# A fused attention and FFN block on one core: last layer-norm step of four units on GpSimd, weight loads behind row transfers, all orders anew

## The reference

```python
qkv = (jnp.einsum('bnd,ed->bne', x, qkv_w) + qkv_b).reshape(b, n, H, 3 * HD)
attn = softmax(einsum('bhqd,bhkd->bhqk', q, k) * SCALE, axis=-1)
x = layernorm(x + (einsum('bnd,ed->bne', out, fc_w) + fc_b + x))
h = silu(tlin(x, w1_w, w1_s)) * tlin(x, w2_w, w2_s)
h = gelu(tlin(h, h1_w, h1_s), approximate=False)
h = gelu(tlin(h, h2_w, h2_s), approximate=False)
x = layernorm(x + tlin(h, w3_w, w3_s))
```

## Time and profile before

| | |
|---|---|
| median of 3 runs | 312.81 us (312.67 to 313.73) |
| the profiled execution | 313.6 us, of which 311.8 are the span from the first to the last instruction |
| TensorE busy | 290.1 us (93%) |
| VectorE busy | 249.6 us (80%) |
| ScalarE busy | 241.4 us (77%) |
| GpSimd busy | 143.4 us (46%) |
| granted TensorE clock, mean | 0.98 |

### The profile page before, as it was taken

The page is one execution under the profiler, slowest core; times in us unless marked ns, Lnnn a source line. Parts: engine busy times, 40 slices in busy tenths (PEclk is TensorE's granted clock), DMA queues, the critical chain, the costliest instruction groups (busy, mean ns, idle before and its releaser), DMA issues.

```text
span 311.8 us, 6746 instructions
## 1 busy us (share of the span) xinstructions
PE 290.1 (93%) x2337; PEld 167.9 (54%) x2337; DVE 249.6 (80%) x561; ACT 241.4 (77%) x458; POOL 143.4 (46%) x255
## 2 busy tenths in 40 slices
PE   8959699999999999999999999998999999999991
PEld 8733254456555546353444363454556568558980
DVE  0669779998989999798899868538998784658993
ACT  2744588898979998999999888989886896984440
POOL 5162679514628991606149816707493290000101
PEclk9979899999999999999999999999999999999996
DMA  5687410045641004403610034450100000010011
GB/s 156 192 149 166 151 37 5 4 65 72 107 68 35 4 0 69 71 5 47 93 52 4 2 55 85 67 78 10 34 4 3 2 3 2 2 36 0 3 34 38
DMA packets 20276, 15.67 MB, mean 50 GB/s; under 512 B 2945, under 2 KB 19090, under 8 KB 20242
## 3 DMA queue, kind: packets, MB, share of 16 engines
q1 hardware_dynamic: 20242, 15.22, 24.9%
HBM read 5.51 MB, written 1.05 MB: 21 GB/s over the span
## 4 chain that ended last, share of the span: by engine, by line
PE 65%; DVE 12%; ACT 8%; SPq 5%; issue 4%; DMA 3%; POOL 0%; POOLq 0%; DVEq 0%; ACTq 0%
PE bank L484 23%; PE bank L524 14%; PE bank L495 8%; PE bank L506 8%; DVE negmax L879 7%; SPq L382 4%; ACT prob L735 4%; PE bank L466 2%; PE bank L548 2%; DMA stack<-mT 2%; PE bank L477 2%; DMA stack<-parts 1%; PE bank L578 1%; PE bank L459 1%; PE bank L565 1%
## 5 line engine op out<-in xcount | busy, mean ns | idle before, releaser
L879 DVE TENSOR_REDUCE negmax<-bank 128x1 f32<-128x512 f32 x256 | 159.8, 682 | 29.9 <-PE bank L495 29.4
L735 ACT ACTIVATE prob<-bank 128x512 f32<-128x512 f32 x256 | 134.0, 618 | 9.1 <-PE bank L506 8.0
L484 PE MATMUL bank<-act,hT 128*128 128x256 f32 (+1 forms) x384 | 71.0, 329 | 0.3 <-DVE negmax L879 0.2
L524 PE MATMUL bank<-prob,v_sb 128*32 128x256 f32 (+1 forms) x768 | 67.4, 458 | 1.2 <-DVE negmax L879 0.9
L484 PEld LDWEIGHTS bank<-act,hT 128*128 128x128 f32 x384 | 55.2, 189 | 11.6 <-issue 3.7
L495 PE MATMUL bank<-stack 64*128 64x512 bf16 x256 | 56.8, 385 | 4.5 <-DMA stack<-parts 3.2
L506 PE MATMUL bank<-stack 64*128 64x256 bf16 (+1 forms) x384 | 55.1, 309 | 3.6 <-DMA stack<-mT 2.8
L802 ACT ACTIVATE h_nat<-bank,hs_all 128x256 f32<-128x256 f32 (+1 forms) x48 | 25.0, 548 | 20.2 <-PE bank L484 19.9
L506 PEld LDWEIGHTS bank<-stack 64*128 64x128 bf16 x384 | 19.6, 94 | 32.1 <-issue 13.5
L524 PEld LDWEIGHTS bank<-prob,v_sb 128*32 128x32 f32 x768 | 21.7, 109 | 26.9 <-issue 16.9
L495 PEld LDWEIGHTS bank<-stack 64*128 64x128 bf16 x256 | 15.9, 94 | 34.3 <-issue 19.7
(11 more groups left out here) (119 smaller groups left out, 357.3 us busy)
## 6 DMA issues: line engine op xcount, KB each, us to landing
stack<-parts SPq DMA_DIRECT2D x64, 128.0 KB, 3.9
x_in<-in_L_attn_x_dram SPq DMA_DIRECT2D x4, 256.0 KB, 3.5
h_nat<-in_L_ffn_h_w_dram SPq DMA_DIRECT2D x1, 1024.0 KB, 7.8
work<-in_L_ffn_h_w_dram SPq DMA_DIRECT2D x1, 1024.0 KB, 6.3
res<-in_L_attn_x_dram SPq DMA_DIRECT2D x4, 256.0 KB, 3.4
work<-in_L_ffn_w_w_dram SPq DMA_DIRECT2D x2, 256.0 KB, 3.4
out_dram<-y SPq DMA_DIRECT2D x4, 128.0 KB, 2.9
out_dram<-y SPq DMA_DIRECT2D x2, 256.0 KB, 2.3
```

Of the source, the lines that this page charges most:

```text
L484: mm = nc.tensor.matmul(dst, w, v, start=first and n == 0, stop=last and n == len(pairs) - 1)
L524: last = nc.tensor.matmul(space("P", pfirst)[at:at + VW, 0:w], v_sb[b % 2][:, kt, of:of + VW], prob[:, t % NP, c * w:(c + 1) * w], start=k ...
L735: nc.scalar.activation(prob[:, n % NP, :], space("T", n)[:, :], ACT.Exp, scale=SCALE).then_inc(emptied("T", n), 1)
L879: nc.vector.tensor_reduce(negmax[:, g % 2, col:col + 1], space("S", n)[:, :], AX.X, ALU.max, negate=True).then_inc(emptied("S", n), 1)
```

## The change

The fifth step of a layer norm becomes a function `normalize`, and a table `NORM` says where it runs: units 0 to 3 on GpSimd (`n1`, `n2` in `POOL_ORDER`), units 4 and 5 on VectorE as before. Its two semaphores get one copy per engine, and `until_norm` waits for the right one; VectorE now waits for it in the first step of the next norm that uses the same rows. `l3` and the second `lh` move behind row transfers. The planner that makes the tables was given measured lengths for FFN pieces, and all five tables are new. The core of the diff (of each table the first line or two):

```diff
 SP_ORDER = """
 lw lh xin vb
-zk zq zk zq*4 zk*6 mrow zq*3 l3 lh mrow xres mrow more xin mrow*2 spread mrow spread*2 xin spread mrow xres mrow*2 spread*2 mrow*2 spread*2 mrow xres
+zk*2 zq*5 zk*6 mrow zq*3 mrow lh mrow l3 more xin mrow*2 xres spread mrow spread*3 xin mrow xres mrow*2 spread*2 mrow spread mrow spread mrow*2
...
 PE_ORDER = """
-K:0 K:1 K:2 K:3 K:4 K:5 K:6 K:7 K:0 x:1 wq:2 q:3 q:4 K:5 wf:6 K:7 wt:0 wt:1 K:2 K:5 K:3 K:7 K:4 K:2 v:5 wt:3 K:7 x:6 wt:4 S:0 S:2 S:1 S:7 S:3 S:5 S:0
+K:0 K:1 K:2 K:3 K:4 x:5 wq:6 K:7 q:0 q:1 wf:2 K:3 K:4 wt:5 wt:6 K:7 K:3 K:0 K:4 K:1 K:7 v:3 K:0 K:4 K:2 wt:1 S:5 S:7 S:6 S:0 S:4 S:2 S:3 S:1 x:5 K:7
...
-H*3 X:5 K:0 H*2 H:7 A:2 A:3 B*2 H A:4 B H A:1 B H*5 H:0 H*7 H:5623 H*7 W:7 H W*3 H H:4105 H*2 Y:6 H*7 K:2 K:3 K:7 W:6 W*3 K:4 Y:1"""
+H*2 H:7 K:3 A:5 B A:6 A:0 H*2 B*2 A:2 B H*5 H:4 H*7 H:3156 H*8 W:7 H H:0243 H*7 W H*2 W*2 W:1 Y:5 W*3 K:6 Y:0 K:2 K:4 K:3 K:7"""
...
-    LN_STEPS = 5
+    LN_STEPS = 4
...
+    NORM = [(0, 0), (0, 0), (0, 0), (0, 0), (1, 1), (1, 1)]
...
+    ON_N = [[[u for u in range(NU) if NORM[u][i] == e] for e in range(2)] for i in range(2)]
...
+        def until_norm(eng, i, u):
+            e = NORM[u][i]
+            eng.wait_ge((x1_ok, y_ok)[i][e], ON_N[i][e].index(u) + 1)
...
                 elif what == "xres":
                     sp.wait_ge(ps_wq, 2)
-                    wait(sp, x1_ok, FIRST[n])
+                    if n:
+                        until_norm(sp, 0, FIRST[n] - 1)
...
+        def normalize(eng, do, e, i, n):
+            u = ON_N[i][e][n]
+            b, t0, nt = UNITS[u]
+            eng.wait_ge(rs_ok[i], u + 1)
+            if i:
+                wait(eng, st_out, 16 * BEFORE[u])
+            elif b > 1:
+                eng.wait_ge(ps_x1T, LAST[b - 2] + 1)
+                until_empty(eng, "Y", LAST[b - 2])
+            dst, done = ((x1[b % 2], x1_ok), (y, y_ok))[i]
+            for t in range(t0, t0 + nt):
+                last = do.tensor_scalar(dst[:, t, :], res[i][:, t, :], mv[i][:, t, 0:1], rstd[i][:, 1, t:t + 1], ALU.subtract, ALU.mult)
+            last.then_inc(done[e], 1)
...
                     dve.wait_ge(resb, b + 1)
+                    if BEFORE[u]:
+                        until_norm(dve, 0, BEFORE[u] - 1)
...
+                elif what in ("n1", "n2"):
+                    normalize(dve, nc.vector, 1, int(what == "n2"), n)
...
+                elif what in ("n1", "n2"):
+                    normalize(pool, nc.gpsimd, 0, int(what == "n2"), n)
```

More of the change, by code:

```diff
@@ L9 @@
 lw lh xin vb
-zk zq zk zq*4 zk*6 mrow zq*3 l3 lh mrow xres mrow more xin mrow*2 spread mrow spread*2 xin spread mrow xres mrow*2 spread*2 mrow*2 spread*2 mrow xres
-out mrow spread*2 mrow spread*2 mrow out xres mrow*3 out*4"""
+zk*2 zq*5 zk*6 mrow zq*3 mrow lh mrow l3 more xin mrow*2 xres spread mrow spread*3 xin mrow xres mrow*2 spread*2 mrow spread mrow spread mrow*2
+spread*2 mrow xres spread*2 mrow*2 xres out mrow out mrow out*4"""
 PE_ORDER = """
-K:0 K:1 K:2 K:3 K:4 K:5 K:6 K:7 K:0 x:1 wq:2 q:3 q:4 K:5 wf:6 K:7 wt:0 wt:1 K:2 K:5 K:3 K:7 K:4 K:2 v:5 wt:3 K:7 x:6 wt:4 S:0 S:2 S:1 S:7 S:3 S:5 S:0
@@ L15 @@
[L15 to L22, removed]
@@ L56, in post_ln_block_kernel @@
+db*2 u h0 u l0 h0 u m l0 h0 l0 u h0 l0 m gh*4 gl*4 p2 m n2 xr gh*2 gl gh*2 gl*3 p1 n1 m h0*3 l0*3 h0 l0 m xr gh*2 gl*2 gh gl gh gl m p1 p2 n2 p1 p2 n2
+p2*2"""
 def post_ln_block_kernel(
@@ L265, in post_ln_block_kernel @@
         rs_ok, ln_step = ([sem(f"{n}{i}") for i in range(2)] for n in ("rs_ok", "ln_step"))
-        x1_ok, y_ok = sem("x1_ok"), sem("y_ok")
+        x1_ok, y_ok = ([sem(f"{n}{e}") for e in range(2)] for n in ("x1_ok", "y_ok"))
         ps_x1T, hi_x1T = sem("ps_x1T"), sem("hi_x1T")
@@ L581, in step @@
                 elif what == "X":
-                    pe.wait_ge(x1_ok, n + 1)
+                    until_norm(pe, 0, n)
                     until_free(pe, "X", n)
@@ L845, in layernorm @@
                     dve.wait_ge(ps_w3T, u + 1)
-                    wait(dve, y_ok, BEFORE[u])
+                    if BEFORE[u]:
+                        until_norm(dve, 1, BEFORE[u] - 1)
                     nc.vector.tensor_tensor(flat(r), space("Y", u)[:, 0:width(u)], flat(x1_b), ALU.add).then_inc(emptied("Y", u), 1)
@@ L857, in layernorm @@
                     last.then_inc(ln_step[i], 1)
-                elif k == 3:
+                else:
                     dve.wait_ge(ln_step[i], 3 * u + 2)
                     nc.vector.tensor_scalar(rstd[i][:, 0, tiles(u)], mv[i][:, tiles(u), 1], EPS, None, ALU.add).then_inc(ln_step[i], 1)
-                else:
-                    dve.wait_ge(rs_ok[i], u + 1)
-                    if i:
-                        wait(dve, st_out, 16 * BEFORE[u])
-                    elif b > 1:
-                        dve.wait_ge(ps_x1T, LAST[b - 2] + 1)
-                    dst, done = ((x1_b, x1_ok), (y, y_ok))[i]
-                    for t in ts:
-                        last = nc.vector.tensor_scalar(dst[:, t, :], r[:, t, :], mv[i][:, t, 0:1], rstd[i][:, 1, t:t + 1],
-                                                       ALU.subtract, ALU.mult)
-                    last.then_inc(done, 1)
             for what, n, _ in walk(DVE_ORDER):
```

57 lines of the change are left out of this document (32 added, 25 removed).

## The result

The changed kernel took **318.11 us** (median of 3 runs, 317.24 to 321.34) where the kernel before took 312.81: ratio 1.0171, 95% interval 1.0102 to 1.0241. It is slower by 1.7%, above the predicted range. The profiled execution took 317.24 us, its span is 315.4.

A forecast was written before the change was run, and what follows sets the result against it. Taken as bound by a pipeline of three nearly full engines (TensorE, VectorE, ScalarE) behind a slow first 36 us. 313.6 - 4.0 - 1.9 - 1.3 - 0.7 = 305.7, less 0.8 to the median: 304.9 us, range 300.0 to 311.0.

The forecast's parts named there:

- (d): Units 0 to 3: 24 last norm steps leave VectorE, sparing 7.5 us; a quarter on the path, -1.9 (ends 0 and -3.8).
- (f): Batch 3's copies: over 6 us earlier, halving VectorE's 2.51 us wait; -1.3 (ends 0 and -2.5).
- (g): Tail: unit 4's FFN pieces and transposes take the place of fillers; -0.7 us (ends 0 and -1.2).
- (h): All other order on TensorE, ScalarE and VectorE, permuted everywhere: 0, with ends -2 and +2 us.
- (a): Start: 46 filler matmuls instead of 62 before the first transposes of x; -1.3 us at the chain's head.
- (b): Start, SP's queue: a second k copy before the q copies takes one issue off the chain; -0.6 us.
- (c): Start: weights behind group 1's row transfer, its T at about 28.5 instead of 35.02; a little over half of 3.85 us.
- rival 5: Start: group 2's row transfer takes the place of group 1's, only the fillers are saved; 311.5 us, chance 0.10.
- (e): GpSimd's norm pieces: 0.30 to 0.46 us each, 0.35 taken, covered by its idle time; 0 on the path.
- Rival 6: GpSimd's norms delay the maxima in three places, 3.7 us, if a piece costs over 0.4 us; 314.6 us, chance 0.08.
- Rival 3: GpSimd and VectorE block each other in SBUF, 0.36 us per piece; 307.3 us, chance 0.06.

The follow-up runs named there:

- the short piece: Changed kernel with GpSimd's last norm step of units 0 to 3 replaced by a copy of the same 128 columns (0.29 us): 312.14 us, ratio 0.9961.
- the start alone: Kernel before with only the new start (two k copies then five of q, weights behind a row transfer, 16 fewer fillers): 308.83 us, ratio 0.9835.
- the two splits: S pieces pulled into long FFN runs: in the changed kernel with x on VectorE, 318.66 us; in the kernel before with the new start, 311.79.

## Why the prediction was wrong

In points of the time before, the change is made of four parts, each the difference of two runs above: the start -1.65; the other orders with the norms on VectorE +2.46 (1.0081 less 0.9835); the norms off VectorE, at 0.29 us a piece, -1.20; the real price of the piece +2.10. That is +1.71, or -5.2, +7.7, -3.8 and +6.6 us. The runs' intervals make them uncertain by 0.3, 0.4, 0.5 and 0.8 points. The second and third hang together: the kernel between them has norm steps put in by hand. Taken as one, the new orders with a quick piece lose 1.26 points, 4 us, against the old orders with the norm on VectorE, where the prediction had a gain of 3.9 ((d), (f), (g) and (h)).

- **(a), (b), (c), the start: right.** First transposes at 5.86 (5.6 forecast), T of group 1 at 28.49 (28.5) with a wait of 0.59 for its row transfer; the only other such wait of T is 0.41, at 88.54. The reason given held too: the last of the three copies of q ahead of that transfer landed at 28.04. Together -5.2 in its own run, where the sum had -4.0 with ends at -1.3 and -5.75. "A shift of its start is carried on, not swallowed" holds for the old orders to 0.3 us. Group 2's row transfer did not take the place of group 1's: rival 5 falls.
- **(d), VectorE spared: right in kind, its size open.** -1.9 with ends 0 and -3.8; the short piece shows -3.8, with the hand-placed steps in it. VectorE was busy 243.1 us (242 forecast).
- **(e), GpSimd's price: the first step that failed.** 0.80 us for 0.35, above the upper end of 0.46, and its cost of 0 on the path held at most for y in the new orders. The bound was carried down from the nearest rows, but none of these had a scalar per partition; such a form with one operation takes 0.60 already, and "nearest the cast, since one tensor is read" chose by what is read, not by what is done. The cover was looked for at m. The place is x: a transpose that TensorE reaches in order, with VectorE's split and the FFN behind it. TensorE stands there 5.4 us longer than with the short piece (5.4 + 0.3 less 0.3), which is most of the 6.6.
- **(f), batch 3's copies: no gain shown.** They were to come over 6 us earlier. SP issues them from 181.79 on, where before it was 182.16; and VectorE's wait of 2.51 has become two, of 1.85 and 1.37 us at 188.95 and 191.01. The stretch around it (row maximum 176 to 224) takes 49.6 us where the start alone takes 48.6. It was not run apart from the orders.
- **(g), the end: no gain that can be told**, where -0.7 was taken with 0 as one end.
- **(h), all other order: the second step that failed.** 0 with ends -2 and +2 was taken; +7.7, or +4.0 with the gain of (d) in it. TensorE's idle time in a stretch, 0.7 to 1.2 us, was taken for the size of what orders can do. But waits also hide in busy time: pipelined pieces that lie over each other less, as in the T rows above. Which moves of the new orders do this stays open.
- **The rivals.** Rival 6 had the right sign, and its point, a price over 0.4 us, was passed, but not its place: TensorE's weight loads wait 2.7 us in all for GpSimd's maxima parts, in the old orders 2.0; the three waits that grew are x's. Rival 3 (the GpSimd copies that it reads beside VectorE's pair, four in 2.28 us from 97.59 on, are in the trace but not in the earlier trace rows): GpSimd's pieces were longer beside VectorE's SBUF work, VectorE's 12 x steps were not there to be hindered, and its price was paid by two or three y pieces. The Trainium skill, SBUF - State Buffer, says in its section on the two sides of the memory that the loser blocks for the whole instruction. Here GpSimd's piece was longer by 0.32 to 0.46 us of 0.79, and none of VectorE's copies beside it took over 0.44: the trace agrees that the two collide, but VectorE did not stand still for a whole piece of GpSimd's. Whether GpSimd stood still for a whole copy it does not show.

The start and (d) as measured are -9.0 us; the prediction's sum was -7.9. That they lie so near is partly luck, since the start and (d) gave more than was taken and (f) and (g) gave nothing that shows. The forecast was one for a kernel with a quick piece and orders as good as the old ones, and this change had neither.

## What to carry to other kernels

Before a step goes to another engine, price the very form (operations, scalars, columns) or bound it by rows of the same form, and then follow its consumer: where an engine that works in order reached it within the extra time, nearly all of that time was on the path here, however idle the new engine was on average. A set of orders that was tuned together is a thing by itself: the three edits here that moved a few pieces inside a set (x later, the two splits) lost 3 to 8 us, and neither kernel that joined two sets kept the lead of its first one. So test a bundle by its parts: its best part alone beat the bundle by 3%.

## What had not been expected of the hardware

TensorE's clock fell after some of the stands, and made them dearer. The run with the transposes of x later, in stretches of 2 us (length, PE, PEld, DVE, ACT, POOL, granted clock, DMA):
```profile
66.00:68.00 2.00, 0.86 (x6) 0.30 (x4) 1.84 (x4) 0.72 (x2) 0.13 (x1) 1.00 0.04 8
68.00:70.00 2.00, 1.31 (x8) 1.05 (x8) 0.81 (x2) 0.47 (x1) 0.00 (x0) 0.80 0.67 80
70.00:72.00 2.00, 1.80 (x8) 1.78 (x8) 0.43 (x2) 0.94 (x3) 0.00 (x0) 0.50 0.83 139
72.00:74.00 2.00, 2.00 (x18) 0.60 (x16) 1.58 (x4) 1.00 (x3) 1.73 (x3) 0.50 0.36 52
74.00:76.00 2.00, 2.00 (x17) 0.95 (x13) 0.89 (x2) 1.64 (x4) 1.11 (x3) 0.50 0.00 0
76.00:78.00 2.00, 2.00 (x16) 1.20 (x15) 2.00 (x7) 1.92 (x5) 0.49 (x1) 1.00 0.00 0
```
After the wait of 1.41 us from 66.95 on the clock fell to its lower level (0.50, which is 1.2 GHz), by the 0.80 of the second row at about 69.2, and stayed there until 76: eight FFN matmuls took 2.04 us there and 1.31 just before. Over the whole profiled execution the mean clock was 0.968, in the changed kernel 0.991. That is a part of why this run lost more than it moved. The changed kernel stood for 1.08 us at 66.90 and its clock did not fall, so a stand does not decide it alone.
